# Records of a four-layer graph network sorted by destination: rows of 64 bytes in device memory in place of 8, and the list read back in four parts

## What is computed

```python
edge_index = stack([src, dst])                                # 200000 edges
x = layernorm(x + L0(x, edge_index))   # two GCN convolutions: segment_sum(h[src] * norm, dst)
x = layernorm(x + L1(x, edge_index))   # GAT: softmax over the edges into each dst, 4 heads
x = layernorm(x + L2(x, edge_attr_3, edge_weight1, edge_index))  # attention by row = src, 8 heads
x = layernorm(x + L3(x, edge_index))   # messages summed by dst, then a linear update
```

## Time and profile before

| | |
|---|---|
| median of 3 runs | 15013.75 us (15009.1 to 15029.12) |
| the profiled execution | 15007.94 us |
| its span, first to last instruction | 15006.1 us |
| busy, share of the span | PE 48%, DVE 53%, POOL 44%, ACT 15% |
| TensorE's granted clock, mean | 0.642 of full speed |
| phases by the barriers in the trace | load to 63; fields and count to about 310; rank 310 to 3118; second scatter 3119 to 6969; gcn1 from 7064; lists from 8454 |

### The profile page before, as it was taken

How to read it: one execution, slowest core, us unless ns; L and a number is a source line. 1 busy time by engine, 2 the same in 40 slices (tenths; PEclk the granted TensorE clock), 3 DMA queues, 4 the chain that set the end, 5 groups by cost and what they waited for, 6 DMA issues and landing times. The chain is left out here.

```text
span 15006.1 us, 180023 instructions
## 1 busy us (share of the span) xinstructions
PE 7250.9 (48%) x37569; PEld 5619.2 (37%) x37570; DVE 7982.7 (53%) x21837; ACT 2322.5 (15%) x6049; POOL 6624.7 (44%) x6504
## 2 busy tenths in 40 slices
PE   5444444411000266653889200026665666666569
PEld 4334333311000266652445100025554555555444
DVE  7555555520000388887020699976665666666631
ACT  0101101000000022210010100001213444444300
POOL 0555555567777400001100277765543555555400
PEclk9555555555555555555889655556676888888789
DMA  0000000010000266664658466666672222222347
GB/s 26 1 1 1 1 1 1 1 31 1 10 18 18 75 201 199 196 187 143 245 215 306 138 203 202 204 178 201 206 189 73 82 83 83 83 82 83 64 165 264
DMA packets 1114463, 1673.21 MB, mean 112 GB/s; under 512 B 287476, under 2 KB 828112, under 8 KB 1075632
## 3 DMA queue, kind: packets, MB, share of 16 engines
q1 hardware_dynamic: 543264, 1032.94, 20.7%
q0 software_dynamic: 234960, 339.86, 9.0%
q10 hardware_dynamic: 335808, 296.39, 6.7%
HBM read 1263.13 MB, written 405.27 MB: 111 GB/s over the span
## 5 line engine op out<-in xcount | busy, mean ns | idle before, releaser
L1317 POOL DMA_INDIRECT big<-tab_h,idx x1664 | 1832.1, 1101 | 2159.2 <-DMA tab_h<-asrc 1293.5
L2145 POOL DMA_INDIRECT big<-tab_kv,idx x1664 | 1592.5, 957 | 1380.9 <-PE banks L2220 488.8
L898 POOL DMA_INDIRECT by_src<-big,h x1568 | 1508.2, 962 | 1198.5 <-DVE h L620 748.7
L1194 DVE SCALAR_TENSOR_TENSOR acc<-acc,h,banks 128x128 f32<-128x128 f32 x3966 | 1082.1, 343 | 1343.6 <-remote 1108.8
L898 POOL DMA_INDIRECT by_dst<-x,h x1456 | 1547.6, 1063 | 496.8 <-issue 462.6
L1419 DVE SCALAR_TENSOR_TENSOR acc<-big,room,acc 128x1280 f32<-128x1280 f32 (+1 forms) x960 | 1378.9, 1525 | 21.6 <-DMA big<-cells 21.6
L1085 PE MATMUL banks<-we2t,idx 128*128 128x8 f32 x3328 | 762.2, 358 | 958.6 <-issue 457.2
L1085 PEld LDWEIGHTS banks<-we2t,idx 128*128 128x128 f32 x3328 | 753.0, 331 | 992.6 <-issue 786.1
L1659 PE MATMUL banks<-big,h 128*128 128x448 f32 x2744 | 1060.3, 547 | 94.6 <-issue 77.7
L2220 PE MATMUL banks<-big,room 128*128 128x136 f32 x3328 | 694.8, 342 | 680.3 <-DVE acc L2317 647.4
L898 POOL DMA_INDIRECT by_dst<-room x112 | 107.2, 957 | 1990.6 <-POOLq L2439 1956.7
(11 more groups left out here) (467 smaller groups left out, 13973.6 us busy)
## 6 DMA issues: line engine op xcount, KB each, us to landing
big<-cells SPq DMA_DIRECT2D x262, 1568.0 KB
cells<-acc SPq DMA_DIRECT2D x1985, 64.0 KB
cells<-acc ACTq DMA_DIRECT2D x1984, 64.0 KB
big<-cells ACTq DMA_DIRECT2D x196, 640.0 KB
head_rows<-big SPq DMA_DIRECT2D x416, 264.0 KB
big<-head_rows SPq DMA_DIRECT2D x208, 528.0 KB
acc<-w_rows SPq DMA_DIRECT2D x208, 512.0 KB
big<-loc_rows SPq DMA_DIRECT2D x208, 256.0 KB
```

Of the source, the lines that this page charges most:

```text
L898: pool.indirect_dma_start(self.target, bass.IndirectOffsetOnAxis(self.slots[:, t:t + 1], axis=0), self.rec[:, t, :], None).then_inc(self.s ...
L1194: dve.scalar_tensor_tensor(k.cells[:, c * SIDE + m, :], before, k.cell_flag[:, bass.ds(j * (2 * SUB) + s * SUB + c * SIDE + m, 1)], cell_b ...
L1317: pool.indirect_dma_start(k.stage[:, m % BODY, :], None, k.tab_h_dram, bass.IndirectOffsetOnAxis(k.idx[:, m:m + 1], axis=0)).then_inc(k.ga ...
L2145: pool.indirect_dma_start(far[:, m % (G * RING), 0:2 * C], None, k.tab_kv_dram, bass.IndirectOffsetOnAxis(k.idx[:, m:m + 1], axis=0)).then ...
```

## The change

`by_dst` gets rows of 16 floats (64 bytes). One column's scatter now takes 16 floats from each partition: the record and the seven that follow it in SBUF, of which only the first two floats are ever used. The fill of `by_dst` grows with it, from two DMAs of 836 KB to eight of 1672 KB, all from one pattern of 4 floats a record (the second pattern and its memset go). The list by destination is read in four DMAs of 3328 KB into two halves of `big` in turn, with DVE's copies of a part between.

```diff
+ROW = 16
-    k.by_dst_dram = dram("by_dst", (P * TD, 2))
+    k.by_dst_dram = dram("by_dst", (P * TD, ROW))
-            rows = k.by_dst_dram.rearrange("(p s r) f -> p s (r f)", p=P, s=2)
-            for s in range(2):
-                act.dma_start(rows[:, s, :], pattern[:, half * 4:half * 6]).then_inc(zero_done, 16)
-            act.wait_ge(zero_done, 64)
+            parts = ROW // 2
+            rows = k.by_dst_dram.rearrange("(p s r) f -> p s (r f)", p=P, s=parts)
+            for s in range(parts):
+                act.dma_start(rows[:, s, :], pattern[:, 0:half * 4]).then_inc(zero_done, 16)
+            act.wait_ge(zero_done, 16 * (2 + parts))
...
-                self.rec[:, t, :], None).then_inc(self.scattered[r], 16)
+                self.flat[:, t * self.fields:t * self.fields + self.row], None).then_inc(self.scattered[r], 16)
...
 def lists_phase(nc, k, which):
-    rec = k.acc[:, 0:T * full].rearrange("p (t f) -> p t f", f=full)
+    full, parts = {"dst": (ROW, 4), "src": (4, 1)}[which]
+    room = {"dst": k.big, "src": k.acc}[which]
+    per = T // parts
+    rec = [room[:, m * per * full:(m + 1) * per * full].rearrange("p (t f) -> p t f", f=full)
+           for m in range(min(parts, 2))]
-            sp.dma_start(rec, source.rearrange("(p t) f -> p t f", p=P)[:, 0:T, :]).then_inc(loaded, 16)
+            for m in range(parts):
+                if m >= 2:
+                    sp.wait_ge(copied, m - 1)
+                sp.dma_start(rec[m % 2], source[:, m * per:(m + 1) * per, :]).then_inc(loaded[m % 2], 16)
-            dve.wait_ge(loaded, 16)
-            dve.tensor_copy(k.idx[:, 0:T], rec[:, :, 0])
-            dve.tensor_copy(k.loc[:, 0:T], rec[:, :, 1])
+            for m in range(parts):
+                dve.wait_ge(loaded[m % 2], 16 * (m // 2) + 16)
+                dve.tensor_copy(k.idx[:, m * per:(m + 1) * per], rec[m % 2][:, :, 0])
+                ins = dve.tensor_copy(k.loc[:, m * per:(m + 1) * per], rec[m % 2][:, :, 1])
+                if which == "dst":
+                    ins = dve.tensor_copy(k.loc_pair[:, m * per:(m + 1) * per], rec[m % 2][:, :, 1])
+                ins.then_inc(copied, 1)
             dve.memset(k.loc[:, T:T + G], PAD)
-            if which == "dst":
-                dve.tensor_copy(k.loc_pair, rec[:, :, 1])
```

More of the change, by code:

```diff
@@ L245, in allocate @@
     xx = k.x[:, :, :].rearrange("p b c -> p (b c)")
-    k.dst_rec = xx[0:EP, 0:2 * EC].rearrange("p (t f) -> p t f", f=2)
+    k.dst_flat = xx[0:EP, 0:2 * EC]
+    k.dst_rec = k.dst_flat.rearrange("p (t f) -> p t f", f=2)
     k.w_f = xx[0:EP, 2 * EC:3 * EC]
@@ L253, in allocate @@
     spare = room[:, 6 * BC * C:6 * BC * C + 3 * TAIL]
+    k.tail_flat = spare
     k.tail_rec = spare[:, 0:2 * TAIL].rearrange("p (t f) -> p t f", f=2)
@@ L327, in _ @@
         def _(act):
-            act.wait_ge(filled, 2)
+            act.wait_ge(filled, 1)
             half = TD // 2
@@ L350, in _ @@
             dve.memset(k.w_f[96:EP, :], 0.0).then_inc(padded, 1)
-            link(dve, dve.memset(pattern[:, 0:half * 6], 0.0))
+            link(dve, dve.memset(pattern[:, 0:half * 4], 0.0))
             p4 = pattern[:, 0:half * 4].rearrange("p (r f) -> p r f", f=4)
-            p2 = pattern[:, half * 4:half * 6].rearrange("p (r f) -> p r f", f=2)
             dve.memset(p4[:, :, 1:2], PAD).then_inc(filled, 1)
-            dve.memset(p2[:, :, 1:2], PAD).then_inc(filled, 1)
             dve.memset(k.ones[:, :], 1.0)
@@ L885, in __init__ @@
         self.target = {"src": k.by_src_dram, "dst": k.by_dst_dram}[key]
-        self.rec = {"src": k.src_rec, "dst": k.dst_rec}[key]
+        self.flat, self.fields, self.row = {
+            "src": (k.src_rec.rearrange("p t f -> p (t f)"), 4, 4), "dst": (k.dst_flat, 2, ROW)}[key]
         self.slots = k.pos[key]
@@ L1287, in lists_phase @@
 def lists_phase(nc, k, which):
-    loaded = k.sem("lists_loaded")
-    full = {"dst": 2, "src": 4}[which]
-    source = {"dst": k.by_dst_dram, "src": k.by_src_dram}[which]
-    rec = k.acc[:, 0:T * full].rearrange("p (t f) -> p t f", f=full)
+    loaded, copied = [k.sem(f"lists_loaded{r}") for r in range(2)], k.sem("lists_copied")
+    full, parts = {"dst": (ROW, 4), "src": (4, 1)}[which]
+    source = {"dst": k.by_dst_dram, "src": k.by_src_dram}[which].rearrange("(p t) f -> p t f", p=P)
+    room = {"dst": k.big, "src": k.acc}[which]
+    per = T // parts
+    rec = [room[:, m * per * full:(m + 1) * per * full].rearrange("p (t f) -> p t f", f=full)
+           for m in range(min(parts, 2))]
     with nc.Block() as block:
@@ L1637, in _ @@
                 scatter = Scatter(k, "dst")
-                scatter.rec, scatter.slots = k.tail_rec, k.tail_pos
+                scatter.flat, scatter.slots = k.tail_flat, k.tail_pos
                 scatter.gpsimd(pool, 0, TAIL)
```

## The result

The changed kernel takes 15105.51 us (median of 4 runs, 15097.17 to 15117.54) against 15011.42 for the kernel before beside it (4 runs, 15002.81 to 15029.12). The ratio is 1.006, 95% interval 1.0046 to 1.0074: **slower by about 94 us, where 1770 less had been forecast**, and above the end of the range (15080). The profiled execution spans 15095.4 us, 89.3 more than before.

The account below looks back on a forecast made before the run. Bound taken: small scattered writes drain at 1.36 to 1.41 us a column against POOL's 1.26, starving other engines. Terms -1682 - 100 - 28 + 8 + 26 = -1776 from 15007.9 gave 13240 us; range up to 15080, likeliest case 13100 to 13600.

Parts of the forecast that it names:

- Part 1: Second scatter phase: 64-byte rows drain faster than POOL issues columns, so cell work runs beside the scatter; -1682 us.
- parts 2 and 3: Backlog relief elsewhere: matmuls beside the first graph layer's tail scatter, -100 us; DVE's remote waits in the rank phase, -28 us.
- point to partial writes: Gathers into SBUF, 512-byte stores to `cells` and SP's slow 4-byte writes, read as showing that small writes drain slowly.
- rival A: Scatters: 64-byte writes drain no faster, since a scattered write from POOL's queue costs whatever its size; 15042 us, chance 0.15.
- Part 4: Rank phase: the 1568 columns of `by_src` are not touched and stay as slow; 0.
- Part 5: Load phase: 12.0 MB more fill, mostly hidden as DMA engines are at 15%; 0 to 28 us, taken +8.
- Part 6: List by destination: reading 13.6 MB for 1.7 takes 36 us for 10; +26 us.
- B: Scatters: drain time grows with bytes, say to 1.6 us a column, and holds POOL; 15340 us, chance 0.06.
- C: Second scatter phase: backlog returns in part beside the stores to `cells`, half of the gain; 14080 us, chance 0.12.

Follow-up runs that it names:

- flight2: Kernel before with at most 2 columns in flight in all three scatters, in place of 24: 15630.09 us against 15752.88 on chip 14 (one execution).
- short_write: Changed kernel with its 64-byte rows, fill and list kept, but only 8 bytes of each row written: 15321.67 us, ratio 1.0047 to kernel before, chip 12.
- gather_dst: Kernel before with 1408 columns of the second scatter turned into gathers from `by_dst` into SBUF: 16936.37 us against 15752.88 on chip 14 (one execution).
- tail2_b: Kernel before with at most two columns in flight in the first graph layer's tail alone: ratio 1.0006 on chip 4; same kernel as tail2, 0.9925 on chip 12.
- flight4: Kernel before with at most 4 columns in flight in all three scatters, in place of 24: 15658.88 us, ratio 0.9937, chip 14.
- after_third: The changed kernel, unedited, timed again on chip 4 against the kernel before at 11591.92 us: 11649.76 us, ratio 1.0062.
- pace1_long: Kernel before with POOL clearing a 128x192 scrap tile ahead of each scatter column: 12276.77 us, ratio 1.06, chip 11; again on chip 4, ratio 1.0625.
- flight8: Kernel before with at most 8 columns in flight in all three scatters, in place of 24: 16026.8 us against 15752.88 on chip 14 (one execution).

## Why the prediction was wrong

**Part 1, the second scatter, and with it parts 2 and 3.** This is the step that failed, with -1682, -100 and -28 on it; all three measured 0 (the scatter 2083.8 us for 2080.6, gcn1's stretch 148.8 for 148.9, the rank phase 5 longer). The chain was: small writes to device memory drain in 1.36 to 1.41 us a column; POOL offers one each 1.26; a backlog grows and starves the others; a wider write drains faster. Runs refute three of its links. The columns that have not landed make no backlog that matters: with two in flight it crawls just as well (flight2). The width does nothing: 8 and 64 bytes are 2 us apart (short_write). It isn't a write: gathers crawl alike (gather_dst). The "drain rates" were read off the crawl itself: 22.4 us is 16 times 1.40, and 1.40 is the same for scatters and gathers and for 8 and 64 bytes, so it is not the time of 128 small writes. That something else is served at 1.40 us a column, and POOL outruns it, is not refuted and not shown. The three rows that "point to partial writes" compared SP's and ACT's queues with POOL's and so varied the issuer together with the size, which rival A had said. Its sentence "what costs is a write to a scattered place from POOL's queue, not its size" is the nearest to what was found, but "write" is too much in it.

What the stage would take without the crawl was priced well, as far as another chip can tell. In tail2_b the cell work and the scatter do run side by side, with stores in 1885 us where part 1 had 1913, and POOL's 1456 columns and 31 gathers in 2045 us (2318.2 to 4363.1), 1.38 us each, within the bounds of 1.26 to 1.46. Only the change doesn't bring it about.

The trace had a row that speaks against part 1, and I used it for the other side: gathers at 1.46 us a column beside loads and stores, without a crawl. I put that down to their writing SBUF. gather_dst writes SBUF too and crawls. Two differences are left: the pace, 1.46 us against 1.26 to 1.40, and the row, 528 bytes against 8. No run separates them.

The Trainium skill, "DMA: Bandwidth & Descriptors", Specifications, gave rival A its ground: below 512 B a read-modify-write. By that rule 64 bytes are as partial as 8. In effect that agrees with what was measured, no gain. Whether transfers under 512 B play a part in the crawl is open: all that crawled, gather_dst's reads of 8 bytes too, were under it. They are not enough to make it, since the same 8-byte rows ran without it in the first graph layer of flight2, flight4 and tail2.

**Part 4, `by_src` 0:** right, up to 5 us.

**Part 5, fill +8:** it was 29, at its upper bound of 28. The error is in the picture of spare capacity: I let the fill use the 85% of the DMA engines that are free from 30 us on the earlier trace rows. But while the fill runs SP needs up to 14 us to issue one load, the phase ends with the chain of these loads, and the free share came behind the fill and moved back with it.

**Part 6, list +26:** right within a microsecond, 35.9 us for 10.7.

**Missing: the cell stage's +23** (22 on each of the other two chips). The prediction took the stores at their old rate. It doesn't go with the width of the write (short_write) or with the crawl (after_third); its cause stays open.

**The rivals.** A was right in its outcome, nothing removed and all additions paid, not in its cause (a write), and off in size: +34 for a measured +94, by 21 in the fill, 23 in the cells, 5 in the rank phase, 6 behind them, and some 5 between the profiled pair and the medians. It had 0.15. B and C had no part in it.

**What the crawl is, as far as the runs go.** It comes while POOL issues indirect DMAs of 128 rows of 8 to 64 bytes back to back, at 1.26 to 1.40 us, on some chips. With POOL held by its landings to a mean of 1.71 us (flight4) or 2.85 and more (tail2, flight2) in the first graph layer, on chips that have it, it is gone. Whether a scatter held to 1.5 us frees the second scatter phase was not seen, as pace1_long met chips without it twice. Why one chip has it and another not, and what it is that POOL's issuing holds up, no run shows.

## What to carry to other kernels

Before a slow stage is put down to the size of a transfer, find two rows that differ in the size and not in the issuing engine; if there are none, run the transfer short in the new layout first. When every engine crawls beside POOL's back-to-back indirect DMAs, on a beat that doesn't follow the data, try to hold POOL by its own landings where its work is hidden anyway: here two columns in flight in one place gave 0.75% on a chip with the crawl and cost nothing on one without. A large fill in the load phase was not free here while another queue still issued loads one by one, though the DMA engines were 85% idle behind it.

## What the runs showed that I had not expected

- The same kernel takes 11590 to 11614 us on two chips and 15011 to 15753 on the others. The rank phase's 1568 scatters take 1983 us on the one kind (333.0 to 2315.8 in tail2_b) and 2691 on the other, at the same 0.96 us for one of POOL's instructions. The second attention layer's 1664 gathers differ too, 2124 us (8577.9 to 10701.6 in tail2_b) and 2752 (11418.0 to 14169.5 in the kernel before), though no "remote" wait of DVE marks that phase.
- In the crawl of the second scatter phase and of the first graph layer most of the gaps over 0.6 us between instructions of ACT, of PE and of SP's queue are multiples of 0.70 us (2.80 between matmuls, 22.4 between copies), whether POOL scatters 8 or 64 bytes or gathers.
- With `by_dst` at 13.6 MB in place of 1.7, the stores of 64 KB to another array took 1.2% longer in each of three series, also where nothing touches `by_dst` meanwhile.
- Single gathers can take 259 to 285 us, with POOL busy all the while: two in flight2 and flight4, three in flight8. The traces of the kernel before have none over 2.4 us.
